# Attention reciprocals as exp(-ln) with one Newton step, and five parts of the step order moved

## The reference, cut to what matters

```python
x = x + attention(layernorm(x), ctx)     # 16 heads of 32; ctx is 128 wide
#   q = xn @ Wq.T ; k, v = split(ctx @ Wkv.T)
#   p = softmax(causal(q @ k.T / sqrt(32))) ; o = p @ v ; o @ Wout.T
x = x + ffn(layernorm(x))                # router logits (512 x 8) per token,
#   softmax over the 8 experts, the best two kept and scaled to sum 1,
#   weights summed over the 512 outputs, eight expert matmuls 512 x 512
```

## Time and profile before

| | us |
|---|---|
| median of three runs (lowest, highest) | 2101.2 (2097.2, 2106.05) |
| profiled execution, its own time | 2104.04 |
| its span, first to last instruction | 2102.3 |
| busy: TensorE, VectorE, ScalarE, GpSimd | 2014.0, 1514.6, 1006.4, 850.9 |
| reciprocals on VectorE, 96 | 116.5 |
| mean granted TensorE clock | 0.974 |

### The profile page before, as it was taken

How to read it: one execution, slowest core, us unless ns; L and a number is a source line. 1 busy time by engine, 2 the same in 40 slices (tenths; PEclk the granted TensorE clock), 3 DMA queues, 4 the chain that set the end, 5 groups by cost and what they waited for, 6 DMA issues and landing times.

```text
span 2102.3 us, 31137 instructions
## 1 busy us (share of the span) xinstructions
PE 2014.0 (96%) x9872; PEld 1519.7 (72%) x9872; DVE 1514.6 (72%) x3300; ACT 1006.4 (48%) x2030; POOL 850.9 (40%) x985
## 2 busy tenths in 40 slices
PE   5899999999997899999999999999999999999999
PEld 3556656666654677777777777778888888888887
DVE  5767777778776667777778777658877778778532
ACT  2544554554443346777666867733433334333300
POOL 3667667667666335434444435202211113111100
PEclk8989999999998999999999999999999999999999
DMA  5444544544454535445455355472322222222110
GB/s 155 117 103 116 146 114 118 137 126 117 119 131 152 194 143 205 179 175 185 170 183 206 146 194 185 153 263 81 110 95 75 83 87 101 100 79 75 60 40 31
DMA packets 99220, 275.85 MB, mean 131 GB/s; under 512 B 13435, under 2 KB 14480, under 8 KB 95030
## 3 DMA queue, kind: packets, MB, share of 16 engines
q1 hardware_dynamic: 94518, 216.16, 32.4%
q10 hardware_dynamic: 4608, 58.72, 8.1%
HBM read 131.67 MB, written 92.27 MB: 107 GB/s over the span
## 4 chain that ended last, share of the span: by engine, by line
PE 81%; DVE 11%; DMA 3%; issue 2%; POOL 1%; SPq 1%; ACT 1%; ACTq 0%; POOLq 0%; DVEq 0%
PE pair L262 21%; PE pair L264 21%; PE pair L263 20%; DVE o_sb L1274 4%; DVE pair L1254 3%; PE ps L648 3%; PE pair L608 3%; PE pair L843 2%; PE pair L635 2%; PE ps L262 2%; PE ps L263 1%; PE ps L264 1%; PE ps L668 1%; DVE nmax L1254 1%; DVE qk L1238 1%
## 5 line engine op out<-in xcount | busy, mean ns | idle before, releaser
L262 PE MATMUL pair<-w_h,hT 128*128 128x512 f32 x1920 | 797.1, 415 | 0.4 <-DVE xb L1581 0.4
L264 PE MATMUL pair<-w_h,hT 128*128 128x512 f32 x1920 | 751.7, 392 | 0.0
L263 PE MATMUL pair<-w_l,hT 128*128 128x512 f32 x1920 | 747.6, 389 | 0.0
L1772 POOL TENSOR_TENSOR logits<-logits,second 128x512 f32<-128x512 f32 x224 | 298.3, 1367 | 607.7 <-DVE second L1460 607.3
L264 PEld LDWEIGHTS pair<-w_h,hT 128*128 128x128 f32 x1920 | 360.6, 188 | 80.3
L263 PEld LDWEIGHTS pair<-w_l,hT 128*128 128x128 f32 x1920 | 361.5, 188 | 74.7
L262 PEld LDWEIGHTS pair<-w_h,hT 128*128 128x128 f32 x1920 | 363.3, 189 | 69.9 <-issue 0.8
L1581 DVE SCALAR_TENSOR_TENSOR xb<-pair,c_now,xb 128x512 f32<-128x512 f32 x256 | 191.7, 749 | 188.7 <-PE pair L264 182.2
L1254 DVE CUSTOM_DVE_ANT_0 pair<-pair,future 128x256 f32<-128x256 f32 (+3 forms) x512 | 242.5, 504 | 113.8 <-PE pair L608 112.6
L996 ACT ACTIVATE pT<-pair,zero 128x1024 f32<-128x1024 f32 (+3 forms) x256 | 203.0, 794 | 246.5 <-PE pair L635 241.3
L608 PE MATMUL pair<-qk_st 96*128 96x256 f32 (+3 forms) x512 | 174.8, 370 | 19.9 <-DVE nmax L1254 15.6
(11 more groups left out here) (161 smaller groups left out, 2830.2 us busy)
## 6 DMA issues: line engine op xcount, KB each, us to landing
logits<-lg_all ACTq DMA_DIRECT2D x32, 1792.0 KB, 7.7
qk_st<-qk SPq DMA_DIRECT2D x384, 128.0 KB, 2.3
lg_all<-ev_a SPq DMA_DIRECT2D x32, 768.0 KB, 5.8
lg_all<-ev_b SPq DMA_DIRECT2D x32, 768.0 KB, 3.2
xb<-x SPq DMA_DIRECT2D x64, 256.0 KB, 3.1
hT_all<-hT SPq DMA_DIRECT2D x32, 512.0 KB, 3.5
hT<-hT_all SPq DMA_DIRECT2D x32, 512.0 KB, 3.7
xt<-in_x SPq DMA_DIRECT2D x8, 1024.0 KB, 5.5
```

Of the source, the lines that this page charges most:

```text
L262: pe.matmul(dst, lh, rh, start=start, stop=False)
L263: pe.matmul(dst, lh, rl, start=False, stop=False)
L264: return pe.matmul(dst, ll, rh, start=False, stop=stop)
L1772: pool.tensor_tensor(logits[t % 2][:, e - 1, :], logits[t % 2][:, e - 1, :], second[:], ALU.subtract)\
```

## The change

The three reciprocals of a step leave VectorE. ScalarE takes ln of the 512 sums and exp of its negative in unit 2 (`inverse`), and VectorE corrects the result r by one Newton step, r (2 - d r), in two operations in unit 3 (`refined`); the last step keeps reciprocals, in two halves (`divided`). A set of activation tables is named ahead of ScalarE's first work. Further: `turn_maxima` goes behind the shifted and the value matmuls of unit 6, and ScalarE's `hi_shift` behind that unit's exp; keys of steps 1 and 2 go from unit 5 to unit 6, behind the turn; block 3 of the last projection goes from step 2, units 4 to 7, to step 3, units 0 to 3 (in all batches but the last, where both blocks stay in step 2), and the splits that must follow it from units 0 and 1 of step 3 to 4 and 5; the residual sum stands behind the unit's maxima; the statistics stand at (step, unit) (1,5), (2,1), (2,5), (3,1) and the normalisations at (2,5), (3,1), (3,5), (3,7).

```diff
--- before.py
+++ after.py
...
@@ -277,24 +277,37 @@
         QUERY = {0: 0, 2: 1, 3: 2, 4: 3}
-        KEY = 5
         VALUE = {0: 0, 2: 1, 3: 2, 4: 3}
         SUMMED = 1
+        STATISTICS = ((1, 5), (2, 1), (2, 5), (3, 1))
+        NORMALISED = ((2, 5), (3, 1), (3, 5), (3, 7))
         LAST_GROUP = {3: 0, 5: 1, 7: 2}
         TURNED = {6: (0, 1), 7: (2, 3)}
         OUT_BUF = (0, 1, 2, 0)
-        DIVIDED = {1: (0, 176), 2: (176, 352), 3: (352, 512)}
+        INVERTED = 2
+        REFINED = 3
+        SCALED = 4
         SPLIT_LATE = (3, 6)
-        SPLIT = {(0, 6): -1, (3, 0): 0, (3, 1): 1, (3, 6): 2}
+        SPLIT = {(0, 6): -1, (3, 4): 0, (3, 5): 1, (3, 6): 2}
         ADDS = 2 * (QB - 1)
 
         def key_bank(c):
 
             return 1 if c in (1, 2) else 0
 
-        def out_block(c, v):
-
-            return 2 * (c - 1) + v // QB, v % QB
+        def key_step(c):
+
+            return 6 if c in (1, 2) else 5
+
+        def out_block(c, v, last):
+
+            if c == 1:
+                return v // QB, v % QB
+            if c == 2 and (v < QB or last):
+                return 2 + v // QB, v % QB
+            if c == 3 and v < QB and not last:
+                return 3, v
+            return None
 
 
...
                     def project(v):
-                        i, chunk = out_block(c, v)
+                        i, chunk = out_block(c, v, last)
...
                     for v in range(UNITS):
-                        out = c in (1, 2) and not first
-                        if v == TURN and (more or c < KC - 1):
-                            turn_maxima(n + 1, c + 1)
+                        out = not first and out_block(c, v, last) is not None
...
@@ -772,6 +783,11 @@
                             last_group(LAST_GROUP[v])
                         if v == TURN and not final:
                             values_of(n, c, b, 0)
+                        if v == TURN and (more or c < KC - 1):
+                            turn_maxima(n + 1, c + 1)
+                        if v == key_step(c) == TURN and ahead:
+                            take(key_bank(c), "K", n + AHEAD)
+                            keys((c + AHEAD) % KC, b if c == 0 else b + 1, key_bank(c))
                         if v == LAST and not final:
                             first_sums(n, more or c < KC - 1)
                             values_of(n, c, b, 1)
@@ -783,7 +799,7 @@
-                        if v == KEY and ahead:
+                        if v == key_step(c) != TURN and ahead:
                             take(key_bank(c), "K", n + AHEAD)
                             keys((c + AHEAD) % KC, b if c == 0 else b + 1, key_bank(c))
...
+            def inverse(n, c):
+
+                act.wait_ge(s["summed"], n + 1)
+                before = n - (0, 3, 3, 2)[c]
+                if some(before):
+                    act.wait_ge(s["o_lo"], before)
+                    act.wait_ge(s["o_hi"], before)
+                o = o_sb[OUT_BUF[c]]
+                act.activation(o[:], d_ps[:], ACT.Ln, bias=zero[:]).then_inc(s["logs"], 1)
+                act.wait_ge(s["logs"], n + 1)
+                act.activation(o[:], o[:], ACT.Exp, bias=zero[:], scale=-1.0).then_inc(s["recips"], 1)
...
+            act.preload_act_table_set("natural_log_exp_and_others")
...
-                        if v == TURN and (more or c < KC - 1):
-                            hi_shift(n + 1)
                         act.wait_ge(s["shifted"], u + 1)
...
                         act.activation(pT[kb][:, pair:pair + 2, :], src[:, :, 0:S - kb * P], ACT.Exp, bias=zero[:])\
                             .then_inc(s["exps"], 1)
+                        if v == TURN and (more or c < KC - 1):
+                            hi_shift(n + 1)
                         if c == 0 and v in VALUE:
...
-                        if v == KEY and ahead:
+                        if v == key_step(c) and ahead:
                             hi_of(n + AHEAD, KH, "k", key_bank(c))
                         if (c, v) in SPLIT and not (first and c == 0) and not (last and (c, v) == SPLIT_LATE):
                             d = SPLIT[c, v]
                             hi_outputs(n - c + d, d % KC, b if d >= 0 else b - 1)
-                        if c == 2 and v in (1, 2, 3, 4) and further:
-                            norm_tokens((b + 2) * QB + v - 1, v - 1)
+                        if v == INVERTED and not (first and c == 0):
+                            inverse(n - 1, (c - 1) % KC)
+                        if (c, v) in NORMALISED and further:
+                            i = NORMALISED.index((c, v))
+                            norm_tokens((b + 2) * QB + i, i)
...
-            def reciprocals(n, c, v, sums=d_ps):
-
-                if v == SUMMED:
-                    dve.wait_ge(s["summed"], n + 1)
-
-                    before = n - (0, 3, 3, 2)[c]
-                    if some(before):
-                        dve.wait_ge(s["o_lo"], before)
-                cols = slice(*DIVIDED[v])
-                dve.reciprocal(o_sb[OUT_BUF[c]][:, cols], sums[:, cols]).then_inc(s["recips"], 1)
+            def refined(n, c):
+
+                dve.wait_ge(s["recips"], n + 1)
+                o = o_sb[OUT_BUF[c]]
+                dve.scalar_tensor_tensor(d_ps[:], d_ps[:], -1.0, o[:], ALU.mult, ALU.mult).then_inc(s["refined"], 1)
+                dve.wait_ge(s["refined"], 2 * n + 1)
+                dve.scalar_tensor_tensor(o[:], d_ps[:], 2.0, o[:], ALU.add, ALU.mult).then_inc(s["refined"], 1)
 
             def scaled(n, c, totals=o_ps):
 
-                dve.wait_ge(s["recips"], (n + 1) * len(DIVIDED))
+                dve.wait_ge(s["refined"], (n + 1) * 2)
                 o = o_sb[OUT_BUF[c]]
                 dve.tensor_tensor(o[:], totals[:], o[:], ALU.mult).then_inc(s["o_ok"], 1)
+
+            def divided(n, c):
+
+                dve.wait_ge(s["summed"], n + 1)
+                dve.wait_ge(s["o_lo"], n - 2)
+                for half in range(2):
+                    cols = slice(half * S // 2, (half + 1) * S // 2)
+                    dve.reciprocal(o_sb[OUT_BUF[c]][:, cols], last_d_ps[:, cols]).then_inc(s["refined"], 1)
...
                     for v in range(UNITS):
                         if v == TURN and (more or c < KC - 1):
                             lo_shift(n + 1)
+                        if v == key_step(c) == TURN and ahead:
+                            lo_of(n + AHEAD, KL, "k", key_bank(c))
-                        if c in (1, 2) and not first and v % QB == QB - 1:
-                            residual(b - 1, out_block(c, v)[0], 0)
                         g, vv = target(c, v)
                         if more or c + g < KC:
                             maxima(n + g, (c + g) % KC, vv)
+                        out = None if first else out_block(c, v, last)
+                        if out and out[1] == QB - 1:
+                            residual(b - 1, out[0], 0)
                         if not (first and c == 0):
-                            if v in DIVIDED:
-                                reciprocals(n - 1, (c - 1) % KC, v)
-                            if v == 4:
+                            if v == REFINED:
+                                refined(n - 1, (c - 1) % KC)
+                            if v == SCALED:
                                 scaled(n - 1, (c - 1) % KC)
                         if QUERY.get(v) == KC - 1 and ahead:
                             lo_of(n + AHEAD, QL, "q", 1)
-                        if v == KEY and ahead:
+                        if v == key_step(c) != TURN and ahead:
                             lo_of(n + AHEAD, KL, "k", key_bank(c))
-                        if c == 1 and v >= QB and further:
-
-                            block_statistics(b + 2, v - QB)
+                        if (c, v) in STATISTICS and further:
+
+                            block_statistics(b + 2, STATISTICS.index((c, v)))
...
-                for v in DIVIDED:
-                    reciprocals(NB - 1, KC - 1, v, last_d_ps)
+                divided(NB - 1, KC - 1)
                 scaled(NB - 1, KC - 1, last_o_ps)
...
                         if (c, v) in SPLIT and not (first and c == 0) and (more or (c, v) != SPLIT_LATE):
                             d = SPLIT[c, v]
                             lo_outputs(n - c + d, d % KC)
-                        if c == 1 and v >= QB and further:
-                            scales(b + 2, v - QB)
+                        if (c, v) in STATISTICS and further:
+                            scales(b + 2, STATISTICS.index((c, v)))
```

2 lines of the change are left out of this document (1 added, 1 removed).

## The result

The changed kernel takes 2109.32 us, the median of 18 runs (2104.88 to 2112.67); the kernel before, run on the same chip, 2101.36 (2097.16 to 2106.05, 18 runs). The ratio is 1.0037, 95% interval 1.0028 to 1.0045: slower, by 8 us. Forecast were 2086 us and a gain; the time lies in the stated range of 2060 to 2115, the direction is wrong. The profiled execution took 2109.9 us by its own time, its span is 2108.2.

What follows compares the result with a forecast made beforehand. Waits between TensorE and VectorE at the turn were taken to bound the attention, the only movable part. Six batches 8.4 us, first batch 7, last 1: 16.5 us, 2104.0 to 2087.5, stated as median 2086; range 2060 to 2115.

Steps and rivals of the forecast that it cites:

- The reciprocals' size on VectorE: Each step: three reciprocals, 3.4 us, give way to two dependent operations, 1.4 us; VectorE relieved of 2.0 us.
- The first batch: No projection there and VectorE bounds all units of step 1: 3.5 us gained in each of steps 1 and 2, 7 us.
- The floor behind the turn: From turn to next step at least 3.6 us: 1.0 to nm_l's end, then 2.6; hidden in steps 1 and 2.
- Rival D: Activation tables alternate on ScalarE, two loads per reciprocal, 2.5 us a step: about 2165 us; chance 0.05.
- rival A: Well filled: ScalarE's order does not bind in step 3, no clock lost; 73.9 us a batch, 2066 us; chance 0.14.
- Step 1: 19.3, step 2: 18.4: Forecast lengths in us of these steps in an undisturbed batch, against 20.75 and 19.7 before.
- ScalarE ... in step 0 I charge 0.2 us: ln and exp take 1.3 us in unit 2, hidden in steps 1 to 3; step 0 pays 0.2 us.
- The fourth block ... all the gain of steps 1 and 2 is eaten in step 3: Projection block moved from step 2 to step 3: step 3 rises from 16.5 to 19.5 us; batch 75.1 against 75.3.
- I take half of the loss as gone: Slow matmuls would lie free in step 3's idle tail: 1.3 us of the clock's 2.5 us a batch gained.
- The test that I had set: Granted clock over 133 to 600 us leaving 0.96 by more than 0.02 would show the clock's part wrong.
- rival C: Clock falls in the tails of steps 2 and 3: 80.1 us a batch, 14 us slower, 2115 us; chance 0.17.
- The last batch 1 us: The last batch was to gain 1 us.

Runs made afterwards that it cites:

- e10: e6 with the keys of steps 1 and 2 back in unit 5, ahead of the turn; 2094.9 us, ratio 0.9964.
- e13: e6 with the turn of the maxima and its rounding back at the head of unit 6; 2101.6 us, ratio 0.9997.
- e6: e3 with projection block 3 back in units 4 to 7 of step 2 and its splits back at (3,0) and (3,1); 2077.1 us, ratio 0.9897.
- e3: The changed kernel with the residual sum put back ahead of the unit's maxima; 2097.1 us, ratio 0.9985.
- e14: e6 with the reciprocals back on VectorE in units 1 to 3, without ln, exp and Newton step; 2090.5 us, ratio 0.9944.
- e1: The kernel before with the new reciprocals alone (ln, exp, Newton step), no step moved; 2088.9 us, ratio 0.9949.
- e11: The changed kernel with only projection block 3 and its splits put back, residual sum still behind the maxima; 2082.2 us, ratio 0.991.
- e7: e3 with the normalisation at (3,5) moved to (3,6), behind nm_h; 2095.5 us, ratio 0.9978.
- e4: The changed kernel with the turn of the maxima and its rounding back at the head of unit 6; 2147.5 us, ratio 1.0224.
- e9: e6 with VectorE's 128x2048 subtractions of the router weights later in the last batch; 2075.1 us, ratio 0.9877.
- e2: The changed kernel with VectorE's three reciprocals in units 1 to 3 as before, all moves kept; 2113.1 us, ratio 1.0056.
- e5: e1 with VectorE's reciprocals in the last step, in two halves in unit 2; 2087.6 us, ratio 0.994.
- e12: e9 with VectorE reciprocals in the last batch's step 3 instead of ln, exp and Newton step; 2072.1 us, ratio 0.9857.
- e8: e1 with the turn and nm_h behind unit 6's value matmuls and exp, nothing else moved; 2093.6 us, ratio 0.9971.

## Why the prediction was wrong, step by step

The forecast was -16.5 us and the profiled executions differ by +5.9 (2104.0 and 2109.9), a miss of 22.4. It divides into batches 1 to 6, 14.6, the last batch, 7.7, and the first, -0.8; 0.8 more lies behind the first router matmul and in no step of mine. Four steps of the prediction failed: who waits for the moved residual sum (with a slip of 0.45 us in step 1's sum and 0.6 us too little in step 0), what the fourth block costs in step 3, that half of the clock's loss would go, and that the last batch would gain.

*What held.* The reciprocals' size on VectorE and the Newton pair (0.72 us apart, 0.69 each; 0.73 forecast). One more table load, 764.2 us in, at no cost: the activation ahead of it ends at 764.20 and the next starts at 765.51, so the whole switch took 1.3 us here, and not the 2.66 that the prediction's estimate counts. The first batch, 7.8 for 7, in part by luck: steps 1 and 2 gained 4.3 and 3.5 us and step 3 1.6, step 0 lost 1.5, and the low clock in it went from 23.9 to 6.8 us, which I had not counted. The floor behind the turn (nm_l's end to the next step 2.6 to 2.7 us in most steps 3, 2.6 forecast; 3.0 and 3.5 in two, where the DMA lands later). The keys (e10), and the order of turn and values in steps 1 and 2 (e13). Unit 4 to the turn: 5.05 and 5.2 us in steps 2 and 1 (5.15), and 5.56 in step 3 of the two batches that keep the clock there (5.45); with a low stretch it is 6.5 to 7.1. Rival D is out, and rival A's 73.9 us a batch is what e6 takes (73.95), though e6 is not the kernel that A was stated for: the room was there, and this version of the change did not reach it.

*"Step 1: 19.3, step 2: 18.4."* 19.76 and 19.1. The residual sum was counted on VectorE, with its 0.6 us, but not who waits for it. The next block of the projection writes the bank that it reads, so TensorE waits in unit 0 of step 2 (0.69 us idle at 481.64) and in unit 4 of step 1. e3 takes that wait out: step 2 at full clock is 18.1. This is the question "who waits for the moved instruction" left unasked, about 1 us in step 2 before any clock. In step 1 it is not the cause: e3 leaves the step at 19.74. There my own addition failed: 5.0 us of work behind the turn, less 1.2, plus the keys' 0.7, are 4.5, and with the turn at 5.15 the tail is 9.65, where I wrote 9.2. Measured is 9.64.

*"ScalarE ... in step 0 I charge 0.2 us."* Step 0 is 18.5 for 17.9, and e14, which takes ln and exp away, has 18.1: units 3 and 4 are 1.99 and 1.80 us as before, instead of 2.09 and 2.15. So the charge was 0.45 rather than 0.2; ln and exp measure 0.68 and 0.72 us, not 0.60. The rest of the 0.6 lies ahead of the turn: it begins 5.08 us behind unit 4, and 4.73 in e14, where I had counted with VectorE's 4.5; e1, with the turn ahead of the value matmuls, has 4.56.

*"The fourth block ... all the gain of steps 1 and 2 is eaten in step 3."* Step 3 came out at the 19.5 us of the forecast; what was wrong is the comparison of the block's price, 1.4 us saved in step 2 for 1.5 paid in units 0 to 3 of step 3, about even. Putting the block back alone (e11) lengthens step 2 by 0.95 us (19.1 at the full clock to 20.05) and shortens step 3 by 3.3 (19.7 to 16.4); that is 2.4 us a batch for the order and 1.8 more for the clock (473.1 - 448.0 is 4.2 a batch). Units 0 to 3 of step 3 give 1.3 of the 3.3 (9.64 to 8.31 in e6), as charged. The other 2 us lie behind unit 4. I had that tail right, 10.0 us for 10.2 measured, and 9.1 for 9.0 in batch 6; but I compared it with the old tail, 8.4, on TensorE alone and never worked out what the new reciprocals, without the block's move, would make of step 3. In e1 its tail is 7.5 us (1.44 + 2.35 + 1.69 + 2.00). VectorE of after and TensorE's wait for it in step 3 of batch 3 (unit 4 begins at 353.66), then VectorE of e11 in the same step (unit 4 at 337.45):

```profile
...
353.73 0.43 DVE L1286 CUSTOM_DVE_ANT_0 pair<-pair,future 128x256 f32<-128x256 f32 x1 [1.11 <-PE pair L621]
...
354.47 0.69 DVE L1322 TENSOR_TENSOR xr<-ps,xr 128x512 f32<-128x512 f32 x1
...
356.80 0.57 PE L621 MATMUL pair<-qk_st 96*128 96x128 f32 x2 [1.31 <-DVE nmax L1286]
...
```
```profile
...
336.78 0.43 DVE L1282 CUSTOM_DVE_ANT_0 pair<-pair,future 128x256 f32<-128x256 f32 x1 [0.21 <-PE pair L617]
...
```

With the block in the step VectorE gets unit 3's scores 0.7 us later against unit 4, since three of the block's matmuls stand ahead of them on TensorE, and then makes the residual sum, 0.6 us at its pitch; from there it runs without a gap to the last maxima, and the turn begins 5.56 us behind unit 4 instead of 4.26. The other 0.5 us is nm_h, which in e11 follows the turn as it should (nm_l ends 1.06 us behind the turn's begin) and in after comes late behind a split and the normalisation at (3,5) (1.57). To that I had given 1.0 us; where the clock is full it cost 0.6 (e7), elsewhere nothing.

*"I take half of the loss as gone."* None of the low clock went: 36.3 us before, 37.5 after. Forecast was that slow matmuls lie for free in TensorE's idle tail behind the turn. But the change also puts the value matmuls ahead of the turn, so that the slow stretch (unit 6 has 24.7 of the 37.5 us) now falls on eight matmuls on the path: 1.94 us for 1.06, turn 1.1 us later than its maxima. At the measured steps the clock costs 78.9 - 76.9 = 2.0 us a batch (76.9: 18.5 + 19.8 + 19.1 + 19.5, the last the mean of five of 19.73 and one of 18.56), before 2.5; forecast 1.2. The test that I had set, a granted clock away from 0.96 over the whole stretch, could not see it: the mean stayed and the place changed. What fell on step 3 in five of six batches now falls on step 2 in five and on step 3 in four. That is rival C's mechanism: with the block gone step 2 idles 1.31 us between its scores, as step 3 did before (0.65 in the earlier trace rows). It had been given 0.17. Its time, 2115, is nearer than mine, but not by its own sum: C counts 5.0 us a batch for the clock, 2.0 were measured, and the 1.8 us by which the steps are longer at the full clock are not in it.

Which condition wakes the low clock is not settled by these runs. What they show: most of it lies in units 5 to 7, where TensorE waits, and mostly goes where the waits are filled. In step 3 before and in e14 it is there (26.0, 27.3 us), in e1 and e6 with the shorter VectorE chain not at all; in step 2 it is there when the projection's block is absent (after 20.5, e3 10.2) and gone when it is back (e6, e11: 0), but for e13 (10.2, with the turn ahead); in step 1 it comes with the idling ahead of the turn in e13 (20.5) and not without (e6 0), yet e4, which has the turn ahead too, has none there. And the same wait of 1.31 us that stands ahead of a low stretch in step 2 of batch 5 (493.04) stands in step 3 of batch 3 (356.80), which kept the full clock.

*"The last batch 1 us."* It lost 6.7. Its last step has a bill of its own that I did not look at: VectorE's subtractions of 128x2048 run beside GpSimd's splits, masks and additions and stretch them to 2.5 us and more. Before had such collisions too; what is new is that VectorE waits for ScalarE's exp, the last two subtractions come 4.2 us later, and the load of the router's first block goes out 5.5 us later (rows under e9). Two ways take part of this back: moving the subtractions (e9, 2.9 us), or the three reciprocals back in units 1 to 3 (e14 38.0 us for 41.2 in e6, e2 39.3 for 42.9 in after). Two reciprocals in unit 2 do little, 0.9 us in e5, and 0.2 in e12, where the subtractions had been moved. How the rest is shared between these no run isolates. 1.6 us of the loss are in steps 0 to 2, where the residual sum stood (e3: 61.0 for 64.4 us).

*In sum over six batches*, by the table: steps at the full clock 1.8 us a batch longer than forecast (76.9 for 75.1: 0.6 in step 0, 0.5 in step 1, 0.7 in step 2) and the clock 0.7 to 0.8 more, 6 x 2.5 = 15 us; the last batch 7.7.

*The effects do not add.* The turn's late place is worth 38 us (e4) or 24.5 (e13) with the keys behind it and costs 5 (e8) with the keys in unit 5. With the block in step 2 and the residual sum ahead the four cases are all there: turn and keys as before 2088.9 (e1), the turn moved alone 2093.6 (e8), the keys moved alone 2101.6 (e13), both 2077.1 (e6); e13 and e6 have the statistics and normalisations moved besides, which e10 and e8 show to matter little. Each move alone loses, the two together gain 12 us. My reading, which no run tests by itself, is that the keys ahead of the turn already fill the wait that the value matmuls would fill. e1 and e2 sum to +1 us and after has +8.

## What to carry to other kernels

When work is taken off an engine, ask for each step whether there was a wait that it filled: a block of matmuls between two waits is cheaper where TensorE would idle than in a step that has room by its own sum, and it can keep the clock up as well (e11: 27 us for one block). Price a moved instruction by who waits for it, not by its length, and when several small moves are made together, test them one at a time: here one good change and two moves that are good together were hidden by two bad ones. With only these two taken back the change gains 1.0%, and with the router weights' subtractions and the last step's reciprocals also moved 1.4% (2072.1 us).

## What the runs showed of the hardware

Two fp32 VectorE subtractions of 128x2048 with both inputs in SBUF hold a GpSimd mask of 0.41 us for 2.46 and an addition of 0.73 for 2.64. The Trainium skill ("SBUF — State Buffer", section "SBUF: two separate sides") says that a VectorE operation with two SBUF inputs and a GpSimd operation that reads SBUF exclude each other for the whole instruction; the trace agrees, each GpSimd operation lasting about one subtraction of 2.5 us.

The lower clock takes the eight value matmuls from 1.06 us to 1.94 and the pitch of a projection matmul from 0.23 to 0.42 us. It followed waits of TensorE between short matmuls, of 1.31 and 1.33 us in the rows at 493.04 and 474.03; the same wait at 356.80 left the clock at its full level. It is worth reading by step: the 36.3 and 37.5 us in two kernels were in different places, at a different price.

The VectorE reciprocal costs 1.25 us for 176 columns where a product of 512 takes 0.68; ln and exp of 512 columns on ScalarE take 0.68 and 0.72 us, with no table load between them.
